# Node marks built tile by tile on VectorE, in the first and the last layer of a graph network

## The chip, the cores and the metric

The kernel runs on one core of a Trainium2 chip. The metric is the device time of one execution in microseconds (us); lower is better. The core's engines work beside each other and meet only at semaphores: TensorE (PE in the profile; PEld is its loading of weights), VectorE (DVE), ScalarE (ACT), GpSimd (POOL), which here issues the indirect DMAs, and SyncE (SP), which issues the others.

## The reference, cut to what matters

Four graph layers run over the same 3125 nodes of width 128 and the same 100000 edges, sorted by destination. Two of them matter here:

```
# layer 0, two steps of:
edge  = concat(h[src], h[dst])
msg   = relu(edge @ mW1 + mb1) @ mW2 + mb2
att   = sigmoid(relu(edge @ aW1 + ab1) @ aW2 + ab2)
agg   = segment_sum(msg * att, dst)          # then a node update
# layer 3, once:
msg   = xW[edge_type, src] * deg_inv[dst]    # 16 relations
out   = segment_sum(msg, dst) + x @ self_loop
```

Layers 1 and 2 use dense blocks of an adjacency matrix that the kernel builds at its start. The change does not touch them.

## The kernel before, in words

Edges lie in tiles of 128, one edge a lane. Four tiles are a quad, and the whole edge list is 202 to 204 quads. In both layers a quad goes through the same steps. GpSimd issues four indirect DMAs, one a tile, each of which fetches 128 rows (one per edge, picked by a list of indices in `stage`) into a `ring` buffer in SBUF. VectorE makes the quad's marks: for every tile a 128x128 matrix `mark` that has a 1 where the lane's destination node, relative to the tile's window (`words[..., D_LOC]`), is the column's number, and 0 elsewhere. TensorE multiplies `mark` (as weights) with the fetched rows and adds to PSUM at the window's columns; this is the segment sum. A semaphore `s_done` counts quads that TensorE has finished and frees their ring slot and mark slot.

`attention_pass` (layer 0, lines 1751 to 1907, run twice, 204 quads each) has a ring of 6 quads. Here VectorE also makes `spread` (L1810), a 128x512 matrix compared from `locs` in bf16 against the lane's number; TensorE multiplies it with the node rows of the destinations (L1871, "expansion", two tiles at a time into one PSUM bank `hid`, two quads ahead of the marks' matmuls); VectorE adds the result to the fetched rows (L1829, one add for two tiles), then forms the attention product of each tile with an accumulator (L1834); ScalarE makes the sigmoid (L1854) and scales the messages (L1860); TensorE sums (L1889, L1891). Because `hid` is one bank, an expansion waits for the add before it, and an add for its expansion. VectorE's order in a quad is: spread of the next quad, marks of this quad, wait for the four DMAs (`s_full`), then add, two products, add, two products. Before each quad TensorE's own sequencer loads 16 register values that say which columns to address (`Where.load`, L1405). ScalarE copies the indices to `stage` when a ring slot's DMAs have landed (L1851), and GpSimd waits for that and for `s_done`.

`last_pass` (layer 3, lines 1631 to 1742, 202 quads) has a ring of 8 quads and far less beside the DMAs: VectorE makes the marks as soon as TensorE has finished with their slot (L1688), and TensorE does four matmuls a quad (L1728).

Both are loops written out by hand, six or eight quads a body. The mark of a quad is one `scalar_tensor_tensor` over 128x512 elements: its inputs are the f32 numbers 0 to 127 (`tile_no`, repeated four times by a step of zero) and the four location words of each lane (repeated 128 times each).

Of the kernel before, what the change touches and what calls it, by code (L numbers as in the profile page):

```python
# [6 lines left out]
F32, I32, BF16, F16 = mybir.dt.float32, mybir.dt.int32, mybir.dt.bfloat16, mybir.dt.float16  # L7
# [3 lines left out]
P = 128  # L11
# [6 lines left out]
QUAD = 4  # L18
# [10 lines left out]
D_LOC, D_SRC, D_T16, D_ROW = 0, 1, 2, 4  # L29
# [1601 lines left out]
def last_pass(k, own, rows, loop, out):  # L1631
# [7 lines left out]
    words, where = k.by_dst, k.where  # L1639
    ring = k.sb("ring", [P, RING * QUAD, D], F32, own)  # L1640
    mark = k.sb("mark", [P, RING, QUAD, P], F32, own)
    stage = k.sb("stage", [P, RING * QUAD], I32, own)
    s_full = [k.sem(f"s_full{q}") for q in range(RING)]
    s_staged, s_mark, s_done, s_go = (k.sem(x) for x in ("s_staged", "s_mark", "s_done", "s_go"))
    s_mm, s_out, s_x, s_dve = (k.sem(x) for x in ("s_mm", "s_out", "s_x", "s_dve"))
# [11 lines left out]
    with nc.Block() as block:  # L1657
        @block.scalar
        def _(eng):
            for q in range(RING):  # L1660
                eng.activation(stage[:, q * QUAD:(q + 1) * QUAD], index(q * QUAD, QUAD), ACT.Copy).then_inc(s_staged, 1)  # L1661
            with eng.Fori(0, bodies) as i:
                for q in range(RING):

                    eng.wait_ge(s_full[q], i * (16 * QUAD) + 16 * QUAD)
                    eng.activation(stage[:, q * QUAD:(q + 1) * QUAD], index(i * body + body + q * QUAD, QUAD),  # L1666
                                   ACT.Copy).then_inc(s_staged, 1)

        @block.gpsimd
        def _(eng):  # L1670
            def quad(i, q):
                eng.wait_ge(s_staged, i * RING + q + 1)

                eng.wait_ge(s_done, i * RING + q + 1)
                eng.sem_inc(s_go, 1)
                for t in range(q * QUAD, (q + 1) * QUAD):
                    eng.indirect_dma_start(ring[:, t, :], None, rows,  # L1677
                                           bass.IndirectOffsetOnAxis(stage[:, t:t + 1], 0)).then_inc(s_full[q], 16)
            every(eng, quad)
            for q in range(RING):  # L1680
                eng.wait_ge(s_full[q], (bodies + (q < rest)) * 16 * QUAD)

        @block.vector
        def _(eng):
            def quad(i, q):
                at = i * body + q * QUAD
                eng.wait_ge(s_done, i * RING + q + 1)
                eng.scalar_tensor_tensor(mark[:, q, :, :], k.tile_no[:, 0:P].unsqueeze(1).to_broadcast([P, QUAD, P]), 0.0,  # L1688
                                         words[:, bass.ds(at, QUAD), D_LOC].unsqueeze(2).to_broadcast([P, QUAD, P]),
                                         ALU.add, ALU.is_equal).then_inc(s_mark, 1)  # L1690

            c = Count(eng, s_dve)
            c.step(eng.tensor_scalar(k.deg[:, :], k.deg[:, :], 1.0, None, ALU.max))
            c.step(eng.reciprocal(k.deg[:, :], k.deg[:, :]))
            for b, c0, n, w0, wn in banks():
                x = k.x[:, w0:w0 + wn, :]
                eng.wait_ge(s_mm, b + 1)
                eng.tensor_tensor(x, x, k.ps[:, FREE, 0:n].rearrange("p (w d) -> p w d", d=D), ALU.add).then_inc(s_x, 1)
            every(eng, quad)

            eng.wait_ge(s_done, RING + NQUADS)
            eng.wait_ge(s_x, NB)
            for b, c0, n, w0, wn in banks():
                for j in range(wn):
                    x = k.x[:, w0 + j, :]
                    last = eng.scalar_tensor_tensor(x, k.ps[:, b, j * P:(j + 1) * P], k.deg[:, w0 + j:w0 + j + 1], x,  # L1706
                                                    ALU.mult, ALU.add)
                last.then_inc(s_x, 1)

        @block.tensor  # L1710
        def _(eng):
            eng.sem_inc(s_done, RING)
            open_banks(k, eng)
            for b, c0, n, w0, wn in banks():
                if b:
                    eng.wait_ge(s_x, b)
                for j in range(wn):
                    last = eng.matmul(k.ps[:, FREE, j * P:(j + 1) * P], k.hT[:, c0 + j * P:c0 + (j + 1) * P], loop[:, :],
                                      start=True, stop=True)
                last.then_inc(s_mm, 1)  # L1720
            tiles = Where(k, eng, where)

            def quad(i, q):
                cols, _ = tiles.load(i * RING + q)
                eng.wait_ge(s_mark, i * RING + q + 1)
                eng.wait_ge(s_full[q], i * (16 * QUAD) + 16 * QUAD)
                for j in range(QUAD):
                    last = eng.matmul(k.psf[:, bass.ds(cols[j], P)], mark[:, q, j, :], ring[:, q * QUAD + j, :], start=False,  # L1728
                                      stop=False, skip_group_check=True)
                last.then_inc(s_done, 1)  # L1730
            every(eng, quad)

        @block.sync
        def _(eng):
            for b, c0, n, w0, wn in banks():
                eng.wait_ge(s_x, NB + b + 1)
                if w0 + wn < NW:
                    eng.dma_start(out[c0:c0 + n, :].rearrange("(w p) d -> p w d", p=P), k.x[:, w0:w0 + wn, :]).then_inc(s_out, 16)
                else:
                    eng.dma_start(out[c0:N, :], k.x[0:TAIL, w0, :]).then_inc(s_out, 16)  # L1740
            eng.wait_ge(s_out, 16 * NB)
# [9 lines left out]
def attention_pass(k, own, rows, here, w_att, b_att):  # L1751
# [8 lines left out]
    mark = k.sb("mark", [P, NQ, QUAD, P], F32, own)  # L1760
    spread = k.sb("spread", [P, NQ, QUAD * P], F32, own)
    locs = k.sb("locs", [P, NQ, QUAD * P], BF16, own)
    stage = k.sb("stage", [P, NQ * QUAD], I32, own)
    dot = k.sb("dot", [P, NQ * QUAD], F32, own)

    att = k.sb("att", [P, NQ * QUAD, 2], F32, own)
# [2 lines left out]
    s_staged, s_mark, s_done, s_go = (k.sem(x) for x in ("s_staged", "s_mark", "s_done", "s_go"))  # L1769
    s_spread, s_exp, s_add, s_dot, s_att, s_msg = (k.sem(x) for x in ("s_spread", "s_exp", "s_add", "s_dot", "s_att", "s_msg"))  # L1770
    s_set = k.sem("s_set")
    words = k.by_dst
# [3 lines left out]
    with nc.Block() as block:  # L1776
# [28 lines left out]
        def _(eng):  # L1805
# [6 lines left out]
            def body(i, last):  # L1812
                for q in range(NQ):
# [4 lines left out]
                    elif not last:  # L1818
                        spread_quad(i + 1, 0, g + 1)
                    eng.wait_ge(s_done, g + 1)  # L1820
                    eng.scalar_tensor_tensor(mark[:, q, :, :], k.tile_no[:, 0:P].unsqueeze(1).to_broadcast([P, QUAD, P]), 0.0,  # L1821
                                             words[:, bass.ds(at, QUAD), D_LOC].unsqueeze(2).to_broadcast([P, QUAD, P]),
                                             ALU.add, ALU.is_equal).then_inc(s_mark, 1)
                    eng.wait_ge(s_full[q], i * (16 * QUAD) + 16 * QUAD)
                    for pair in range(2):
                        t = q * QUAD + pair * 2
# [3 lines left out]
                        for j in (pair * 2, pair * 2 + 1):  # L1830
# [3 lines left out]
                            eng.scalar_tensor_tensor(ring[:, t, D:W2], ring[:, t, D:W2], 0.0, w_att[:, :], ALU.max, ALU.mult,  # L1834
                                                     accum_out=dot[:, t:t + 1]).then_inc(s_dot, 1)
            eng.memset(att[:, :, 1], 1.0).then_inc(s_set, 1)
            eng.sem_inc(s_add, 1)
            spread_quad(0, 0, 0)
            with eng.Fori(0, bodies - 1) as i:
# [578 lines left out]
```

## Time and profile before

| | |
|---|---|
| time, median of 3 runs | 7433.94 us |
| lowest and highest | 7425.34 and 7442.86 us |
| span of the profiled execution, first to last instruction | 6780.1 us |
| own time of the profiled execution | not given with the profile; the median is 653.8 us above the span |
| TensorE busy (PE) | 5024.0 us, 74% of the span |
| VectorE busy | 3111.1 us, 46% |
| GpSimd busy | 2431.9 us, 36% |
| ScalarE busy | 1789.9 us, 26% |
| mean granted clock of TensorE | 0.873 of full speed |
| indirect DMAs of GpSimd | 1632 in the two attention passes, 808 in the last pass |

The profile was taken of one execution. Busy shares are averages over very different stages: the attention passes lie from 1040 to 2117 us and from 2203 to 3254 us, the last pass from 5724 to 6763 us, the layers between them from 3254 to 5724 us. A stage is read by who waits for whom inside it, and by what an engine does between two of its instructions.

### The profile page before, as it was taken

Reading aid. Unit: us, or ns where it says so; the run is one execution under the profiler, and the core shown is the slowest. Engines: PE = TensorE matmul, PEld = TensorE weight load, DVE = VectorE, ACT = ScalarE, POOL = GpSimd, SP = SyncE. Lnnn points to the kernel's source line nnn. Section 1 sums busy time; section 2 is a strip of 40 time slices with the busy share of each in tenths; the row PEclk is TensorE's granted clock in tenths of the full one; section 3 lists DMA queues with packets and bytes.
Section 4 is the critical chain, followed back from the end, with each engine's and each line's share of the span. In section 5 each row is a group of like instructions: output and inputs, shape, how many; then the busy total and the mean of one; then the engine's idle time right before and its main releaser. Section 6 shows DMA issues by size and latency. Waiting matters only on the chain. (4 is left out here: it accounts for less than half of the span.)

```text
span 6780.1 us, 95615 instructions
## 1 busy us (share of the span) xinstructions
PE 5024.0 (74%) x29088; PEld 3414.4 (50%) x29089; DVE 3111.1 (46%) x7292; ACT 1789.9 (26%) x4343; POOL 2431.9 (36%) x2473
## 2 busy tenths in 40 slices
PE   2557767777777777777798999999999997443443
PEld 1435556666665676666544444444444444333333
DVE  6889986666664666666565212112112114111111
ACT  2019983444443444444201001001011012000000
POOL 0000006777773777777100000000000001777776
PEclk7569998999999999999899999999999998555555
DMA  2019984444443444444483553553554524211122
GB/s 79 1 47 328 328 279 133 128 121 125 124 121 80 133 128 130 123 129 126 138 304 131 194 192 133 194 193 131 194 180 146 194 97 167 52 51 51 51 51 55
DMA packets 416540, 942.73 MB, mean 139 GB/s; under 512 B 61857, under 2 KB 272982, under 8 KB 406230
## 3 DMA queue, kind: packets, MB, share of 16 engines
q1 hardware_dynamic: 312150, 672.91, 29.4%
q0 software_dynamic: 104192, 267.02, 14.8%
q8 instruction: 144, 2.36, 0.1%
q14 instruction: 54, 0.44, 0.0%
HBM read 735.13 MB, written 204.56 MB: 139 GB/s over the span
## 5 line engine op out<-in xcount | busy, mean ns | idle before, releaser
L1799 POOL DMA_INDIRECT ring<-rows,stage x1632 | 1629.5, 998 | 1138.4 <-ACT stage L1846 642.0
L1677 POOL DMA_INDIRECT ring<-rows,stage x808 | 792.3, 981 | 2716.8 <-ACT stage L1661 2470.9
L1324 PE MATMUL ps<-strip,trans_part 128*128 128x512 f16 (+1 forms) x8232 | 1606.4, 356 | 23.3 <-DVE trans_part L1241 23.3
L1871 PE MATMUL ps<-here,spread 128*128 x3264 | 949.0, 414 | 545.5 <-DVE spread L1810 283.9
L1324 PEld LDWEIGHTS ps<-strip,trans_part 128*128 128x128 bf16 x8232 | 756.5, 98 | 928.2 <-issue 77.4
L1871 PEld LDWEIGHTS ps<-here,spread 128*128 128x128 f32 x3264 | 569.9, 194 | 662.2 <-issue 615.5
L1829 DVE TENSOR_TENSOR ring<-ring,ps 128x512 f32<-128x512 f32 x816 | 560.6, 687 | 699.3 <-PE ps L1871 540.9
L1728 PE MATMUL ps<-ring,mark 128*128 128x128 f32 x1616 | 414.9, 438 | 612.3 <-DMA ring<-rows,stage 610.7
L1889 PE MATMUL ps<-ring,mark 128*128 128x128 f32 x3264 | 695.0, 300 | 0.0
L1728 PEld LDWEIGHTS ps<-ring,mark 128*128 128x128 f32 x1616 | 357.3, 326 | 669.9 <-issue 669.9
L1233 DVE TENSOR_TENSOR trans<-ps,be 128x512 f32<-128x512 f32 x96 | 66.4, 692 | 1186.4 <-PE ps L1314 1186.4
L1889 PEld LDWEIGHTS ps<-ring,mark 128*128 128x128 f32 x3264 | 572.3, 196 | 45.0
L1688 DVE SCALAR_TENSOR_TENSOR mark<-tile_no,by_dst 128x512 f32<-128x512 f32 x202 | 142.8, 711 | 842.5 <-PE ps L1728 842.4
L1860 ACT ACTIVATE ring<-ring,att 128x128 f32<-128x128 f32 x1632 | 521.4, 390 | 13.3
L1891 PEld LDWEIGHTS ps<-att,mark 128*128 128x128 f32 x3264 | 509.0, 197 | 0.0
L1891 PE MATMUL ps<-att,mark 128*128 128x2 f32 x3264 | 467.8, 213 | 0.0
L1278 ACT ACTIVATE trans_part<-trans 128x512 bf16<-128x512 f32 x100 | 62.9, 629 | 1428.9 <-DVE trans L1233 1366.6
L1834 DVE SCALAR_TENSOR_TENSOR ring<-ring,w_att 128x128 f32<-128x128 f32 x1632 | 414.4, 291 | 28.2
L1854 ACT ACTIVATE att<-dot,b_att 128x4 f32<-128x4 f32 x408 | 121.5, 298 | 1139.7 <-DVE ring L1834 1139.7
L881 ACT ACTIVATE piece<-ps 128x1024 f16<-128x1024 f32 x375 | 303.0, 888 | 24.6 <-PE ps L845 24.6
L1666 ACT ACTIVATE stage<-by_dst 128x4 int32 x200 | 41.6, 208 | 988.7 <-DMA ring<-rows,stage 988.7
L1821 DVE SCALAR_TENSOR_TENSOR mark<-tile_no,by_dst 128x512 f32<-128x512 f32 x408 | 277.4, 680 | 0.0
(332 smaller groups left out, 5093.7 us busy)
## 6 DMA issues: line engine op xcount, KB each, us to landing
strip<-adj SPq DMA_DIRECT2D x392, 800.0 KB, 4.3
adj<-piece SPq DMA_DIRECT2D x120, 640.0 KB, 4.0
locs<-loc_rows SPq DMA_DIRECT2D x420, 128.0 KB, 3.1
ahead<-ahead_piece SPq DMA_DIRECT2D x125, 320.0 KB, 4.1
back<-back_piece SPq DMA_DIRECT2D x125, 320.0 KB, 4.5
sheet<-ahead SPq DMA_DIRECT2D x25, 1600.0 KB, 7.4
sheet<-back SPq DMA_DIRECT2D x25, 1600.0 KB, 7.2
ring<-rows,stage POOLq DMA_INDIRECT x2440, 2.5
```

The costliest lines, as they stand in the source:

```text
L881: eng.activation(piece[:, g % PIECES, :, unit[0] * P:(unit[0] + size) * P].rearrange("p t (e c) -> p t e c", c=HN), psf[:, n % 2 * 2 * BAN ...
L1324: last = eng.matmul(k.ps[:, b, 0:cols], part[:, (step * NW + w) % TABLES, m, t * D:(t + 1) * D], strip[:, at % RING, c0:c0 + cols], start= ...
L1677: eng.indirect_dma_start(ring[:, t, :], None, rows, bass.IndirectOffsetOnAxis(stage[:, t:t + 1], 0)).then_inc(s_full[q], 16)
L1728: last = eng.matmul(k.psf[:, bass.ds(cols[j], P)], mark[:, q, j, :], ring[:, q * QUAD + j, :], start=False, stop=False, skip_group_check=True)
L1799: eng.indirect_dma_start(ring[:, t, :], None, rows, bass.IndirectOffsetOnAxis(stage[:, t:t + 1], 0)).then_inc(s_full[q], 16)
L1821: eng.scalar_tensor_tensor(mark[:, q, :, :], k.tile_no[:, 0:P].unsqueeze(1).to_broadcast([P, QUAD, P]), 0.0, words[:, bass.ds(at, QUAD), D ...
L1829: eng.tensor_tensor(ring[:, t:t + 2, :], ring[:, t:t + 2, :], hid, ALU.add).then_inc(s_add, 1)
L1834: eng.scalar_tensor_tensor(ring[:, t, D:W2], ring[:, t, D:W2], 0.0, w_att[:, :], ALU.max, ALU.mult, accum_out=dot[:, t:t + 1]).then_inc(s_ ...
L1860: eng.activation(ring[:, t, 0:D], ring[:, t, 0:D], ACT.Relu, scale=att[:, t, 0:1]).then_inc(s_msg, 1)
L1871: last = eng.matmul(hid[:, j, :], spread[:, q, t * P:(t + 1) * P], here[:, bass.ds(cols[t] * 2, W2)], start=True, stop=True)
L1889: eng.matmul(k.psf[:, bass.ds(now[j], D)], mark[:, q, j, :], ring[:, q * QUAD + j, 0:D], start=False, stop=False, skip_group_check=True)
L1891: done = eng.matmul(k.psf[:, bass.ds(scalar[j], 2)], mark[:, q, j, :], att[:, q * QUAD + j, :], start=False, stop=False, skip_group_check= ...
```

## The change

Each pass gets a 128x128 bf16 copy of the numbers 0 to 127, `lanes`, made once before its loop. The mark of a quad is then made by four `tensor_scalar` instructions, one a tile, that compare `lanes` with the tile's location word as a per-partition scalar. The output stays f32, and the semaphore `s_mark` is raised once, by the fourth.

```
 # last_pass
+    lanes = k.sb("lanes", [P, P], BF16, own)
-                eng.scalar_tensor_tensor(mark[:, q, :, :], k.tile_no[:, 0:P].unsqueeze(1).to_broadcast([P, QUAD, P]), 0.0,
-                                         words[:, bass.ds(at, QUAD), D_LOC].unsqueeze(2).to_broadcast([P, QUAD, P]),
-                                         ALU.add, ALU.is_equal).then_inc(s_mark, 1)
+                for j in range(QUAD):
+                    last = eng.tensor_scalar(mark[:, q, j, :], lanes[:, :], words[:, bass.ds(at + j, 1), D_LOC], None, ALU.is_equal)
+                last.then_inc(s_mark, 1)
...
+            c.step(eng.tensor_copy(lanes[:, :], k.tile_no[:, 0:P]))
 # attention_pass
+    lanes = k.sb("lanes", [P, P], BF16, own)
-                    eng.scalar_tensor_tensor(mark[:, q, :, :], k.tile_no[:, 0:P].unsqueeze(1).to_broadcast([P, QUAD, P]), 0.0,
-                                             words[:, bass.ds(at, QUAD), D_LOC].unsqueeze(2).to_broadcast([P, QUAD, P]),
-                                             ALU.add, ALU.is_equal).then_inc(s_mark, 1)
+                    for j in range(QUAD):
+                        marked = eng.tensor_scalar(mark[:, q, j, :], lanes[:, :], words[:, bass.ds(at + j, 1), D_LOC], None,
+                                                   ALU.is_equal)
+                    marked.then_inc(s_mark, 1)
...
+            eng.tensor_copy(lanes[:, :], k.tile_no[:, 0:P]).then_inc(s_set, 1)
+            eng.wait_ge(s_set, 2)
```

On VectorE, one quad of the attention loop stands in the program before as follows (ISA rows are the sequencer's address arithmetic).

```order
L1809 ISA
L1810 TENSOR_SCALAR spread<-locs,lane 128x512
L1821 ISA
L1821 SCALAR_TENSOR_TENSOR mark<-tile_no,by_dst 128x512
L1828 REGISTER_ALU
L1829 TENSOR_TENSOR ring<-ring,ps 128x512
```

The same stretch of VectorE in the changed program, where lines have moved by three or four:

```order
L1812 ISA
L1813 TENSOR_SCALAR spread<-locs,lane 128x512
L1825 ISA
L1825 TENSOR_SCALAR mark<-lanes,by_dst 128x128
L1825 ISA
L1825 TENSOR_SCALAR mark<-lanes,by_dst 128x128
L1825 ISA
L1825 TENSOR_SCALAR mark<-lanes,by_dst 128x128
L1825 ISA
L1825 TENSOR_SCALAR mark<-lanes,by_dst 128x128
L1832 REGISTER_ALU
L1833 TENSOR_TENSOR ring<-ring,ps 128x512
```

The marks keep their place between the spread and the first add; one instruction with one address computation becomes four with one each.

On VectorE at the start of the last pass's loop, before the change (`deg` and `x` belong to what precedes the loop):

```order
L1693 TENSOR_SCALAR deg<-deg 128x25
L1694 RECIPROCAL deg<-deg 128x25
L1698 TENSOR_TENSOR x<-x,ps 128x512 x6
L1698 TENSOR_TENSOR x<-x,ps 128x128
L1651 UNCONDITIONAL_BRANCH
L1651 ISA
L1688 ISA
L1688 SCALAR_TENSOR_TENSOR mark<-tile_no,by_dst 128x512
```

The same place on VectorE in the changed program:

```order
L1694 CAST lanes<-tile_no 128x128
L1695 TENSOR_SCALAR deg<-deg 128x25
...
L1652 ISA
L1690 ISA
L1690 TENSOR_SCALAR mark<-lanes,by_dst 128x128
L1690 ISA
L1690 TENSOR_SCALAR mark<-lanes,by_dst 128x128
L1690 ISA
L1690 TENSOR_SCALAR mark<-lanes,by_dst 128x128
L1690 ISA
L1690 TENSOR_SCALAR mark<-lanes,by_dst 128x128
```

The copy to `lanes` stands ahead of the loop, and the four comparisons stand where the one stood. No other engine's order changes.

## Rows read from the trace of the kernel before

**Rows 1.** Groups by line; after the bar: busy us, mean ns; idle before, by releaser.

```profile
L1799 POOL DMA_INDIRECT ring<-rows,stage x1632 | 1629.5, 998 | 1138.4 <-ACT stage L1846 642.0 <-issue 496.2 <-PE ps L1891 0.3
L1677 POOL DMA_INDIRECT ring<-rows,stage x808 | 792.3, 981 | 2716.8 <-ACT stage L1661 2470.9 <-issue 245.6 <-PE ps L1728 0.3
...
L1821 DVE SCALAR_TENSOR_TENSOR mark<-tile_no,by_dst 128x512 f32<-128x512 f32 x408 | 277.4, 680 | 0.0
...
L1688 DVE SCALAR_TENSOR_TENSOR mark<-tile_no,by_dst 128x512 f32<-128x512 f32 x202 | 142.8, 711 | 842.5 <-PE ps L1728 842.4
```

**Rows 2.** Busy by engine in the two attention passes; first number the length.

```profile
1040.00:2117.00 1077.00, 794.21 (x4832) 712.62 (x4831) 701.62 (x2427) 440.79 (x1283) 827.70 (x816) 0.97 0.46 124
2203.00:3254.00 1051.00, 795.16 (x4832) 713.82 (x4831) 697.35 (x2428) 436.26 (x1284) 801.75 (x816) 0.97 0.48 128
```

**Rows 3.** Single lines' instructions: ns minimum/median/maximum, first and last start in us.

```profile
L1799 POOL DMA_INDIRECT ring<-rows,stage x1632: 942/946/1475, 1040.7 to 3252.6; - x182
L1677 POOL DMA_INDIRECT ring<-rows,stage x808: 940/944/1462, 5724.4 to 6761.7; - x162
```

**Rows 4.** Timeline of an attention quad: start, length in us, instruction, [idle before].

```profile
2003.92 1.13 PE L1871 MATMUL ps<-here,spread 128*128 x4 [1.49 <-DVE spread L1810]
...
2008.23 0.58 DVE L1810 TENSOR_SCALAR spread<-locs,lane 128x512 f32<-128x512 bf16 x1
...
2008.74 0.67 DVE L1821 SCALAR_TENSOR_TENSOR mark<-tile_no,by_dst 128x512 f32<-128x512 f32 x1
2008.87 1.36 POOL L1799 DMA_INDIRECT ring<-rows,stage  x1 [0.30 <-issue]
...
2010.51 0.69 DVE L1829 TENSOR_TENSOR ring<-ring,ps 128x512 f32<-128x512 f32 x1 [1.10 <-DMA ring<-rows,stage]
```

**Rows 5.** Timeline of two attention quads in a later stretch.

```profile
2726.91 0.28 DVE L1834 SCALAR_TENSOR_TENSOR ring<-ring,w_att 128x128 f32<-128x128 f32 x1
2727.00 1.02 POOL L1799 DMA_INDIRECT ring<-rows,stage  x1 [0.30 <-issue]
...
2727.72 0.68 DVE L1821 SCALAR_TENSOR_TENSOR mark<-tile_no,by_dst 128x512 f32<-128x512 f32 x1
...
2727.74 1.13 PE L1871 MATMUL ps<-here,spread 128*128 x4 [1.02 <-issue]
...
2728.91 0.69 DVE L1829 TENSOR_TENSOR ring<-ring,ps 128x512 f32<-128x512 f32 x1 [0.50 <-PE ps L1871]
...
2732.06 0.48 DVE L1810 TENSOR_SCALAR spread<-locs,lane 128x512 f32<-128x512 bf16 x1
2732.07 0.95 POOL L1799 DMA_INDIRECT ring<-rows,stage  x1 [0.30 <-issue]
...
2732.66 1.12 PE L1871 MATMUL ps<-here,spread 128*128 x4 [1.00 <-DVE spread L1810]
```

**Rows 6.** Timeline of VectorE and GpSimd where a spread and its marks meet a DMA.

```profile
1358.48 0.48 DVE L1810 TENSOR_SCALAR spread<-locs,lane 128x512 f32<-128x512 bf16 x1
1358.72 1.06 POOL L1799 DMA_INDIRECT ring<-rows,stage  x1 [0.30 <-issue]
1358.87 0.69 DVE L1821 SCALAR_TENSOR_TENSOR mark<-tile_no,by_dst 128x512 f32<-128x512 f32 x1
```

**Rows 7.** Timeline of the last pass, VectorE's marks and the DMAs beside them.

```profile
6298.02 0.69 DVE L1688 SCALAR_TENSOR_TENSOR mark<-tile_no,by_dst 128x512 f32<-128x512 f32 x1 [4.22 <-PE ps L1728]
6298.07 1.46 POOL L1677 DMA_INDIRECT ring<-rows,stage  x1 [0.30 <-issue]
...
6303.54 0.76 DVE L1688 SCALAR_TENSOR_TENSOR mark<-tile_no,by_dst 128x512 f32<-128x512 f32 x1 [4.83 <-PE ps L1728]
6303.58 0.94 POOL L1677 DMA_INDIRECT ring<-rows,stage  x1 [0.30 <-issue]
```

**Rows 8.** Timeline: 25 consecutive 128x128 tensor_scalars elsewhere in the program.

```profile
98.59 4.99 DVE L1448 TENSOR_SCALAR h<-h,stat 128x128 f32<-128x128 f32 x25
```

**Rows 9.** The sequencer's address step ahead of each mark, from the marks' line.

```profile
L1821 DVEq FUSED_REGOPS  x396: 69/69/81, 1043.1 to 3220.8; - x198
```

## The prediction

> **What bounds the kernel now.** I read the busy shares by stage first, then the groups by line, then the timeline inside a quad. The page gives TensorE 74% of the span, but the change lies only in the two attention passes and the last pass, so those are read alone.
>
> In the attention passes GpSimd never rests. It has 816 DMA instructions in each pass, busy 827.70 and 801.75 us [rows 2], and idles 496.2 us over 1629 "issue" gaps, 0.304 us each [rows 1]. 827.70 + 816 x 0.304 = 1076 us against a pass of 1077 us, and 801.75 + 248 = 1050 against 1051 [rows 2]. So the length of a pass is the sum of GpSimd's serial instructions; whatever makes one of them longer makes the pass longer. The last pass is the same: 792.3 + 245.6 = 1037.9 us [rows 1] against 5724.4 to 6761.7 plus the last 0.9, which is 1038 us [rows 3].
>
> What makes them longer? The median instruction takes 0.946 us in the attention passes, but the mean is 0.998; in the last pass 0.944 against 0.981 [rows 1, 3]. The excess is 1629.5 - 1632 x 0.946 = 85.6 us and 792.3 - 808 x 0.944 = 29.5 us, together 115 us. The timeline shows where it sits. In [rows 4] the mark starts at 2008.74 and runs to 2009.41; a DMA instruction starts 0.13 us after the mark's start and takes 1.36 us, 0.41 too long. It starts 2008.87, so the mark ends 0.54 us into it: the DMA instruction seems to want something 0.54 - 0.41 = 0.13 us after its start and gets it when the mark ends. In [rows 7] the mark starts 0.05 us before the DMA instruction, ends 0.64 into it, and the excess is 1.46 - 0.94 = 0.52, again 0.12 short of the overlap. When the mark starts 0.04 us ahead, the DMA instruction is normal (0.94) and the mark is the one that is longer, 0.76 instead of 0.69 [rows 7]. So it is a lock: who comes first holds it, and VectorE holds it for its whole instruction. A 128-wide product that ends 0.19 us into a DMA instruction costs it 0.07 (1.02) [rows 5], which fits the same rule.
>
> The quad of [rows 4] repeats. The first add waits for the DMAs (1.10 us idle), so VectorE follows GpSimd at a fixed distance, the mark always falls on the start of a DMA instruction, and a quad takes about 5.4 us instead of 4 x 1.25 = 5.0. In other stretches, as [rows 5], TensorE sets the pace: expansions start at 2727.74 and 2732.66, 4.92 us apart, and the add waits for TensorE.
>
> **What the change does to this.** *The train of four.* Twenty-five 128x128 tensor_scalars take 4.99 us [rows 8]. With one of them 0.28 long, they start (4.99 - 0.28) / 24 = 0.196 us apart. That row is f32 to f32. I take it for bf16 to f32 too, since the bf16 spread over 512 takes 0.48 [rows 5, 6] against 0.68 for the f32 mark over 512 [rows 1]: it has a faster mode already. So a train takes 3 x 0.196 + 0.28 = 0.87 us instead of 0.68. Lower bound: 0.48, the bf16 spread of the same total width [rows 6]. Upper bound: each as costly as that whole spread, three at 0.40 apart (0.24 from the spread's start to the DMA's and 0.15 on to the mark's, [rows 6]) plus 0.48, 1.68 us. The sequencer's address step of 0.069 us each [rows 9] fits under 0.196. I take 0.87, the row nearest in shape.
>
> The Trainium skill (VectorE: DVE Perf Modes, the section on the trn2 errata) gives 58 cycles plus the elements over the mode's factor at 0.96 GHz. By that estimate four instructions of 128 in a doubled mode would take 0.51 us and one of 512 in plain mode 0.59, so the train would be the shorter one. The measured 0.196 apart says otherwise, and the measurement decides.
>
> *What it costs VectorE.* 0.19 us more per quad, 610 quads. In a quad paced by TensorE the mark starts at 2727.72 and the add at 2728.91 [rows 5], 1.19 us of room against a train of 0.87; in a quad paced by GpSimd 1.77 us [rows 4]. In the last pass VectorE idles over 4 us a quad [rows 7]. So the addition is hidden behind TensorE's expansion and the DMAs. If the room were gone (the upper bound of 1.68), a TensorE-paced quad would be 0.49 us later: that end is kept in the range only through its small chance. Who waits for the marks themselves is TensorE's sum two quads later, which is in no hurry.
>
> *What it gives GpSimd.* The lock is now held for one instruction of 0.28 us. In the locked quad the first of the four starts 0.13 before the DMA instruction [rows 4], ends 0.15 into it, and costs 0.15 - 0.13 = 0.02 instead of 0.41. In the last pass, 0.05 ahead, it ends 0.23 into it and costs 0.10 instead of 0.52. Between two back-to-back VectorE instructions GpSimd does get in: in [rows 6] the spread ends 0.24 into the DMA instruction, the mark has been started by then, and the excess is only 1.06 - 0.95 = 0.11, the rule for the spread's end alone.
>
> *Attention.* Not all of the 85.6 us is the marks'; spreads and products keep theirs (0.11 in [rows 6], 0.07 in [rows 5]). And TensorE is close behind: five quads at 4.92 and one with a longer gap for the loop's branch (1.49 against 1.00, [rows 4, 5]) make (5 x 4.92 + 5.41) / 6 = 5.00 us, the same as GpSimd's 5.00. Two queues of equal pace lose a little to each other. I take 5.07 us a quad where it is (1077 + 1051) / 408 = 5.22 now: 408 x 5.07 = 2068, so 60 us less. Bounds: 85 if everything goes, 20 if TensorE and jitter take most of it.
>
> *Last pass.* 29.5 us at about 0.5 a hit are some 59 hits in 202 quads. At 0.10 or less each they leave 6: 23 us less. Bounds 15 and 29.
>
> *The copies.* `lanes` is made three times in all (twice in the attention passes, once in the last), each under 0.3 us by the single instructions above, plus a wait: 1 us more.
>
> Sum: -60 - 23 + 1 = -82 us. The profiled execution gives no own time; its span of 6780.1 would become 6698, and the median of the runs, 7434, stands 654 us above the span for reasons that the change doesn't touch. I forecast 7352 us.
>
> **The rivals.** *One, slower: the train acts as one hold.* If GpSimd did not get in between the four, the hold would last 0.87: in the locked quad the train ends 0.74 into the DMA instruction and costs 0.61 instead of 0.41, and it is hit 0.87 / 0.68 = 1.28 times as often. 115 x 0.61 / 0.41 x 1.28 = 219 us, 104 more than now, 7538 us. For it: the four are issued with nothing between them. Against it: [rows 6]. It decides once the mean excess per quad passes 115 / 610 = 0.19 us.
>
> *Two, slower: the faster mode blocks more of a DMA instruction than the old one did.* The mark moves from an f32 form with two tensor inputs to the form of the spread. If GpSimd cannot do the later part of its work while such an instruction runs, each train would lengthen the DMA instruction that it lies on wherever it falls. Priced at 0.4 us in each of 610 quads, as a locked one costs today, that is 244 us, 129 more than now, 7563 us. Against it: a spread that runs from 2732.06 to 2732.54, over the first half of the DMA instruction of 2732.07, leaves it at 0.95 [rows 5].
>
> The Trainium skill (SBUF — State Buffer, "Who interferes with whom") speaks for it: a two-port instruction of VectorE and a GpSimd instruction exclude each other entirely, whichever starts first, while one with two SBUF inputs excludes only GpSimd's reads; and it warns that GpSimd can't write DMA descriptors meanwhile. By that rule the new form would contend where the old one did not. Of the first half of the rule the trace shows the part with two inputs: 1.46 against 0.94 in [rows 7].
>
> *Three, faster but little: TensorE takes over in the attention passes at once*, so that only the last pass gains: -22 us, 7412 us. For it: 5.00 against 5.00. Against it: the 5.4 us quads of [rows 4] leave TensorE 0.45 us of room each (the expansion was finished, the add waited for the DMA).
>
> *Four, no change: the excess is not the marks'* but belongs to whatever VectorE runs there, and returns with the four. 7434 us. Against it: the same mark moved by 0.09 us against the DMA changes it from 1.46 to 0.94 [rows 7].
>
> **How the numbers follow.** The forecast 0.65; rival one 0.06; two 0.06; three 0.14; four 0.09. Faster by over 0.2% (15 us, about what a measurement of this kernel can tell from no change): the forecast and three, 0.79. Within 0.2%: rival four and a little, 0.10. Slower: 0.11. The range goes from 7322 (both excesses gone, 7434 - 115 = 7319, nearly) to 7428, which takes in rival three and the start of four.
>
> **What would show it.** GpSimd's DMA instructions: mean near 0.96 in the attention passes and 0.95 in the last, hardly any above 1.2 us. The trains about 0.87 us long. Passes of about 1034 us each and 1015 us. The share of adds that wait for TensorE rises, and that of adds that wait for DMAs falls. Wrong if DMA instructions stay at 1.3 and more under the trains (rivals one and two, told apart by whether the train's first or any of them is at the start), if the DMA mean falls but GpSimd begins to wait for TensorE (rival three), or if the trains last over 1.2 us and adds begin right behind them.

## The result, and the profile after

The changed kernel takes 7494.8 us, median of 5 runs, against 7433.2 for the kernel before: ratio 1.0070, 95% interval 1.0054 to 1.0087. It is slower by 0.7% (the medians alone differ by 62 us, 0.8%); I had forecast 1.1% faster, in a range that ends at 7428.

The profiled execution of the changed kernel took 7465.9 us, its span is 7464.0. So a span stands 2 us below its time, not 654. The profile of the kernel before (6780.1 us) was therefore of an execution some 650 us shorter than those that were timed. The chip that each of them ran on is not on record.

Groups by line of the changed kernel, the columns as in [rows 1], which they answer:

```profile
L1802 POOL DMA_INDIRECT ring<-rows,stage x1632 | 1563.3, 958 | 1764.5 <-issue 1111.6 <-ACT stage L1852 643.5 <-ACT stage L1857 7.3
L1678 POOL DMA_INDIRECT ring<-rows,stage x808 | 765.5, 947 | 2867.5 <-ACT stage L1662 2467.7 <-issue 398.3 <-PE ps L1730 1.5
...
L1825 DVE TENSOR_SCALAR mark<-lanes,by_dst 128x128 f32<-128x128 bf16 x1632 | 363.4, 294 | 0.0
...
L1690 DVE TENSOR_SCALAR mark<-lanes,by_dst 128x128 f32<-128x128 bf16 x808 | 170.8, 294 | 939.0 <-remote 697.0 <-issue 161.2 <-PE ps L1730 80.4
```

GpSimd's DMA instructions are shorter than in [rows 1], as forecast: 0.998 to 0.958 and 0.981 to 0.947 us in the mean. But its idle "issue" time in the attention passes is now 1111.6 us where it was 496.2: it waits, and so it no longer sets the pace. Its instructions (940/946/1203 ns, the answer to [rows 3]) now spread from 1041.1 to 3812.6 us:

```profile
L1802 POOL DMA_INDIRECT ring<-rows,stage x1632: 940/946/1203, 1041.1 to 3812.6; - x182
L1678 POOL DMA_INDIRECT ring<-rows,stage x808: 938/944/1076, 6281.2 to 7445.7; - x162
```

The busy time in the same stretches as [rows 2] says it again: 656 DMAs in the first where all 816 had fitted.

```profile
1040.00:2117.00 1077.00, 725.09 (x3850) 646.47 (x3851) 581.53 (x2424) 342.63 (x1027) 628.35 (x656) 0.85 0.36 100
2203.00:3254.00 1051.00, 724.93 (x3743) 632.43 (x3745) 553.04 (x2257) 336.27 (x986) 558.84 (x584) 0.84 0.34 95
```

The longest waits of VectorE (columns: engine, line, waited for: us in total, times, longest) name a releaser that the table of before did not have. The profile writes "remote" where a semaphore's event fits the end of no instruction on record; this program runs on one core, so no other core can be meant:

```profile
DVE mark L1690 <- remote: 697.0, 53, 20.8
DVE ring L1833 <- remote: 606.8, 123, 8.0
```

And the timeline of an attention quad, the counterpart of [rows 4], shows one of them:

```profile
2000.42 0.88 DVE L1825 TENSOR_SCALAR mark<-lanes,by_dst 128x128 f32<-128x128 bf16 x4
...
2001.10 1.02 POOL L1802 DMA_INDIRECT ring<-rows,stage  x1 [0.30 <-issue]
...
2002.44 1.13 PE L1877 MATMUL ps<-here,spread 128*128 x4
...
2006.25 0.94 POOL L1802 DMA_INDIRECT ring<-rows,stage  x1 [0.30 <-issue]
2008.95 0.69 DVE L1833 TENSOR_TENSOR ring<-ring,ps 128x512 f32<-128x512 f32 x1 [6.11 <-remote]
...
2009.78 1.00 POOL L1802 DMA_INDIRECT ring<-rows,stage  x1 [2.59 <-issue]
2009.78 2.07 PE L1877 MATMUL ps<-here,spread 128*128 x4 [5.43 <-DVE ring L1833]
```

The train of four takes 0.88 us. It ends 0.20 us into the DMA instruction of 2001.10 and costs it 1.02 - 0.95 = 0.07: the forecast's rule, for the new form too. But then the expansion of 2002.44, which should be done by 2003.6, is reported done at 2008.93 (the semaphore's own time in the trace), and VectorE, GpSimd and the next expansion stand behind it. The granted clock falls to the lower of its two levels, 1.2 GHz, at 2008.38, after TensorE has run nothing for 4.0 us, and the next expansion takes 2.07 instead of 1.13 us. I call this a hold of TensorE.

How many there are takes care to count, because this trace also lacks records. It keeps 669 of the expansions' some 820 semaphore events. For 116 of the 816 expansions the event came over 2 us after the end and before the next expansion's end: those are late. For 155 no event of their own is on record: since the next expansion waits for this one's add, its event can't come later than that, so it is missing. 271 expansions with no event within 2 us are thus 116 late ones and 155 gaps in the record. 115 adds waited over 3 us, in the median 26 us apart, which agrees with the 116. VectorE's adds lack events too (191 of 816), but none that is on record is over 1 us late: it is TensorE that is held.

### The profile page after: what moved, and what is told of

Its sections match the earlier page's. It is cut to its first block and busy times, and to the rows that moved or that the text cites. A ratio compares the mean times of both kernels' runs of the same rounds, so it can differ in the third digit from the quotient of the medians.

```text
span 7464.0 us, 99233 instructions
## 1 busy us (share of the span) xinstructions
PE 5262.1 (70%) x29085; PEld 3589.3 (48%) x29089; DVE 3199.8 (43%) x9125; ACT 1770.8 (24%) x4343; POOL 2339.0 (31%) x2473
## 5 line engine op out<-in xcount | busy, mean ns | idle before, releaser
L1802 POOL DMA_INDIRECT ring<-rows,stage x1632 | 1563.3, 958 | 1764.5 <-issue 1111.6
L1877 PE MATMUL ps<-here,spread 128*128 x3264 | 1114.1, 472 | 864.3 <-DVE ring L1833 612.2
L1678 POOL DMA_INDIRECT ring<-rows,stage x808 | 765.5, 947 | 2867.5 <-ACT stage L1662 2467.7
L1877 PEld LDWEIGHTS ps<-here,spread 128*128 128x128 f32 x3264 | 664.8, 226 | 993.8 <-issue 923.0
L1730 PE MATMUL ps<-ring,mark 128*128 128x128 f32 x1616 | 417.1, 407 | 707.4 <-issue 663.0
L1895 PE MATMUL ps<-ring,mark 128*128 128x128 f32 x3264 | 773.8, 327 | 0.0
L1730 PEld LDWEIGHTS ps<-ring,mark 128*128 128x128 f32 x1616 | 326.8, 284 | 797.7 <-issue 796.2
L1895 PEld LDWEIGHTS ps<-ring,mark 128*128 128x128 f32 x3264 | 651.5, 222 | 66.6
L1690 DVE TENSOR_SCALAR mark<-lanes,by_dst 128x128 f32<-128x128 bf16 x808 | 170.8, 294 | 939.0 <-remote 697.0
L1897 PEld LDWEIGHTS ps<-att,mark 128*128 128x128 f32 x3264 | 571.3, 219 | 0.0
L1897 PE MATMUL ps<-att,mark 128*128 128x2 f32 x3264 | 503.8, 224 | 0.0
L1825 DVE TENSOR_SCALAR mark<-lanes,by_dst 128x128 f32<-128x128 bf16 x1632 | 363.4, 294 | 0.0
```

What stands on the lines that cost most here:

```text
L1678: eng.indirect_dma_start(ring[:, t, :], None, rows, bass.IndirectOffsetOnAxis(stage[:, t:t + 1], 0)).then_inc(s_full[q], 16)
L1802: eng.indirect_dma_start(ring[:, t, :], None, rows, bass.IndirectOffsetOnAxis(stage[:, t:t + 1], 0)).then_inc(s_full[q], 16)
L1825: marked = eng.tensor_scalar(mark[:, q, j, :], lanes[:, :], words[:, bass.ds(at + j, 1), D_LOC], None, ALU.is_equal)
L1877: last = eng.matmul(hid[:, j, :], spread[:, q, t * P:(t + 1) * P], here[:, bass.ds(cols[t] * 2, W2)], start=True, stop=True)
L1895: eng.matmul(k.psf[:, bass.ds(now[j], D)], mark[:, q, j, :], ring[:, q * QUAD + j, 0:D], start=False, stop=False, skip_group_check=True)
L1897: done = eng.matmul(k.psf[:, bass.ds(scalar[j], 2)], mark[:, q, j, :], att[:, q * QUAD + j, :], start=False, stop=False, skip_group_check= ...
```

## The experiments

Ratios are against the kernel before on the same chip, with 95% intervals. The chips have numbers; 4, 5, 7, 11 and 13 came up, each at one time only. "Late" and "without a record" are counted as above.

**Where the loss lies: before again, and each half of the change alone.** On chip 4. `b1_before` is the kernel before unchanged; `b2_att_only` has the diff's lines in `attention_pass` alone, `b3_last_only` those in `last_pass` alone:

```
# b2: attention_pass; b3: last_pass
-    eng.scalar_tensor_tensor(mark[:, q, :, :], <tile_no x4>, 0.0, <words x128>, ALU.add, ALU.is_equal)
+    for j in range(QUAD):
+        eng.tensor_scalar(mark[:, q, j, :], lanes[:, :], words[:, bass.ds(at + j, 1), D_LOC], None, ALU.is_equal)
```

> The kernel before, unchanged. The changed kernel's trace (span 7464 us) has what the shown trace of before (span 6780 us, against a median of 7434) lacks: VectorE standing still for some 3 to 8 us every 26 us of an attention pass, between two records, with nothing to wait for (123 adds, 607 us in all). Theory A (the stalls are a state of the execution and not of the change: the shown trace was of an execution that had none, the timed executions of before have them too): this trace has a span near 7430 us, attention passes of about 1330 us each instead of 1077 and 1051, and stalls of VectorE in them. Theory B (the change brings the stalls): the span is near 6780 us again with passes near 1060 us, and the 650 us between span and time lie outside the span.

> Only the attention passes make their marks tile by tile; the last pass is as before. Theory A1 (instruction supply: VectorE's stalls come after a fixed number of its instructions, and the attention loop now has 6 more instructions in each quad): this one alone carries most of the change's +61 us, +40 to +70 us. Theory A2 (the loss lies in the last pass): within 15 us of before, or faster by the 60 us forecast for the attention passes.

> Only the last pass makes its marks tile by tile; attention is as before. In it VectorE goes from 3 to about 9 instructions a quad. Theory A1 (stalls counted by instructions): slower by up to 60 us if the last pass' stalls grow with its instructions, since each stall there is not hidden; the original forecast, which knew no stalls: 23 us faster.

The kernel before took 6798.0 us here, and its copy 6784.3 (0.9978, 0.9954 to 1.0002): the same kernel that was timed at 7433. Its trace has a span of 6816.2 for a run of 6817.9, and no "remote" wait. So theory A's stalls did not show, nor did theory B's 650 us outside the span; what differs is the chip, or the time at which it was used. The attention half took 6711.2 us (0.9869, 0.9851 to 0.9887), the last-pass half 6753.0 (0.9940, 0.9915 to 0.9964). Theories A1 and A2 both failed here in their losses: both halves gain, 87 and 45 us (24 to 58 by the second's interval) against the 60 and 23 forecast. DMA instructions in the attention half:

```profile
L1800 POOL DMA_INDIRECT ring<-rows,stage x1632 | 1559.3, 955 | 1137.8 <-ACT stage L1850 641.2 <-issue 474.9 <-ACT stage L1855 20.1
L1677 POOL DMA_INDIRECT ring<-rows,stage x808 | 791.7, 980 | 2714.8 <-ACT stage L1661 2468.8 <-issue 245.7 <-PE ps L1728 0.3
```

The attention group is at 955, the untouched last pass still at 980.

**Both halves, on a chip without holds.** On chip 5, the changed kernel and the one before, both as they are.

> The changed kernel, unchanged, beside the kernel before on the same chip. The runs with before at 6798 us had the attention passes alone at 0.987 and the last pass alone at 0.994 of before, without VectorE's stalls. Theory C1 (the two parts add up and the result of 1.007 belongs to executions with stalls, in which before takes 7433 us): where before takes about 6800 us, this one takes 0.981 of it, some 6670 us; where before takes about 7430, 1.007 of it and its trace has the stalls. Theory C2 (both parts together bring the stalls, neither does alone): about 7490 us even where before takes 6800.

> The kernel before, for its trace. Theory C1: if it takes about 7430 us here, its trace has VectorE stalls of 4 to 6 us in the attention passes as the changed kernel's had, and fewer than its 123; if about 6800, none. Theory C2: no stalls at any time.

6673.3 against 6808.1 us, ratio 0.9796 (0.9780 to 0.9812). C1 holds, C2 falls. The first fence is the changed kernel, the second the kernel before, both by line:

```profile
L1802 POOL DMA_INDIRECT ring<-rows,stage x1632 | 1558.8, 955 | 1137.2 <-ACT stage L1852 640.6 <-issue 476.8 <-ACT stage L1857 19.5
L1678 POOL DMA_INDIRECT ring<-rows,stage x808 | 763.2, 945 | 2713.2 <-ACT stage L1662 2467.3 <-issue 245.6 <-DMA ring<-rows,stage 0.3
L1833 DVE TENSOR_TENSOR ring<-ring,ps 128x512 f32<-128x512 f32 x816 | 560.9, 687 | 538.4 <-PE ps L1877 529.5 <-DMA ring<-rows,stage 8.1
```

```profile
L1799 POOL DMA_INDIRECT ring<-rows,stage x1632 | 1640.2, 1005 | 1137.3 <-ACT stage L1846 640.9 <-issue 496.5
L1677 POOL DMA_INDIRECT ring<-rows,stage x808 | 804.2, 995 | 2713.4 <-ACT stage L1661 2467.5 <-issue 245.3 <-PE ps L1728 0.3
L1829 DVE TENSOR_TENSOR ring<-ring,ps 128x512 f32<-128x512 f32 x816 | 560.6, 687 | 707.2 <-PE ps L1871 516.8 <-DMA ring<-rows,stage 190.3
```

GpSimd's busy time fell by 1640.2 - 1558.8 + 804.2 - 763.2 = 122 us, and the time by 135. Adds waited 8.1 instead of 190.3 us for DMAs. No expansion is late or without a record, in either trace.

**Which part of the change does it.** On chip 7: four f32 instructions (`d1`), one with bf16 numbers (`d2`), two f32 of 256 (`d3`), and the changed kernel (`d4_after`), in both passes.

```
# d1 (n = 1) and d3 (n = 2), in place of the tensor_scalar
+    for j in range(0, QUAD, n):
+        eng.scalar_tensor_tensor(mark[:, q, j:j + n, :], <tile_no x n>, 0.0, words[:, bass.ds(at + j, n), D_LOC]..., ALU.add, ALU.is_equal)
# d2
+    eng.scalar_tensor_tensor(mark[:, q, :, :], lanes[:, :].unsqueeze(1).to_broadcast([P, QUAD, P]), 0.0, <words x128>, ALU.add, ALU.is_equal)
```

> The change's splitting alone: four 128-wide scalar_tensor_tensors in f32 instead of one of 512, no bf16 and no doubled mode. Theory D1 (a DMA instruction is held up by whichever VectorE instruction with two SBUF inputs runs when it starts, until that one ends, so only the length of one instruction counts): GpSimd's DMA mean falls to about 0.957 us in attention and 0.947 in the last pass as with the changed kernel, ratio to before 0.979 to 0.984 where before takes about 6800 us. Theory D2 (the gain comes from the bf16 input or the doubled mode): ratio near 1.00. Where before takes about 7430 us, this one has the changed kernel's instruction count and takes 1.00 to 1.02 of before under the theory that the stalls go with VectorE's instructions.

> The change's bf16 lane numbers alone: one 512-wide scalar_tensor_tensor that reads lanes in bf16. Theory D1: the instruction stays at about 0.68 us and so does the hold: ratio 0.995 to 1.005, DMA means near 1.01 and 0.99 as before. Theory D2: 0.98. Instruction count as before, so where before takes about 7430 us also 1.00.

> Two 256-wide scalar_tensor_tensors a quad. Each lasts about 0.42 us. Theory D1: started 0.05 us ahead of a DMA instruction, one costs 0.42 - 0.05 - 0.13 = 0.24 instead of 0.52 us, and 0.16 instead of 0.41 in the locked attention quad, so a bit over half of the changed kernel's gain: ratio 0.987 to 0.991 where before takes about 6800. Where before takes about 7430 it adds 2 VectorE instructions (one with its address step) a quad instead of 6, and stalls less than the changed kernel.

> The changed kernel once more on the chip of these three, as their measure: 0.980 of before where before takes about 6800 us, 1.007 where it takes about 7430.

This chip is of the other kind: before took 7392.1 us. d1 1.0048 (1.0030 to 1.0065), d2 1.0007 (0.9995 to 1.0018), d3 1.0034 (1.0020 to 1.0049), the changed kernel 1.0048 (1.0030 to 1.0066). The bf16 input alone does nothing; splitting alone, without the faster mode, costs what the whole change costs. Every trace has holds: 109 to 123 late expansions (133 to 189 more without a record), 115 of them with the single instruction of d2. So the holds are not brought by VectorE's instruction count, as I had thought when I wrote A1; d3, which was to have fewer than the changed kernel, has 123 against 114. To read the DMA instructions one needs the kernel before on such a chip. Its attention passes, unchanged, are in `f1_no_fetch` on chip 13 (the last experiment). The groups are d2's, d1's and then f1's:

```profile
L1802 POOL DMA_INDIRECT ring<-rows,stage x1632 | 1593.5, 976 | 1672.9 <-issue 1026.0 <-ACT stage L1851 646.0 <-PE ps L1896 0.9
...
L1824 DVE SCALAR_TENSOR_TENSOR mark<-lanes,by_dst 128x512 f32<-128x512 bf16 x408 | 279.2, 684 | 0.0
```

```profile
L1804 POOL DMA_INDIRECT ring<-rows,stage x1632 | 1565.0, 959 | 1700.9 <-issue 1055.3 <-ACT stage L1855 640.7 <-ACT stage L1860 3.4
...
L1827 DVE SCALAR_TENSOR_TENSOR mark<-tile_no,by_dst 128x128 f32<-128x128 f32 x1632 | 366.0, 285 | 0.0
```

```profile
L1798 POOL DMA_INDIRECT ring<-rows,stage x1632 | 1595.9, 978 | 1702.9 <-issue 1057.8 <-ACT stage L1845 644.2 <-PE ps L1890 0.9
```

GpSimd waits over 1000 us in all three. With holds the DMA instruction of the kernel before is 0.978 us in the mean, not 1.00, and 83 of 1632 last over 1.2 us instead of 199 on chip 5: VectorE and GpSimd meet less often. One long instruction with bf16 leaves it there (0.976), four short f32 ones bring it to 0.959, as the changed kernel does on the same chip (0.960). So D1 holds against D2 for the DMA instruction, though not for the ratio of 0.98, since no chip without holds came up for these. D1's size for d3 was missed: two instructions of 256 were to give over half of the gain, and the mean is 0.976, as with one, although only 7 DMA instructions last over 1.2 us against d2's 72. Why is open.

**The train moved away from the first add.** On chip 11.

```
 # attention_pass, marks of the changed kernel
-    for j in range(QUAD):
+    for j in range(2):                      # between spread and first add
...
+    if pair == 0:                           # behind the first add's two products
+        for j in (2, 3):
+            marked = eng.tensor_scalar(mark[:, q, j, :], lanes[:, :], words[:, bass.ds(at + j, 1), D_LOC], None, ALU.is_equal)
+        marked.then_inc(s_mark, 1)
```

> The changed kernel, but in the attention passes only two of the four comparisons stay between the spread and the first add; the other two stand behind the first add's two products, where VectorE waits 0.76 us for the second expansion. On chip 7, where TensorE is held for some 5 us again and again and GpSimd is not the bound, the changed kernel took 1.005 of before, and 109 first adds started right behind the marks against 84 with one instruction. Theory E1 (there the loss is the longer train ahead of those adds): the train ahead of the add falls from 0.87 to 0.48 us, below the single instruction's 0.68, so this version takes 0.996 to 1.000 of before where before takes about 7400 us, 20 to 50 us less than the changed kernel. Theory E2 (the loss comes with more instructions or more starts of them, wherever they stand): 1.005 again. Where before takes about 6800 us GpSimd's DMAs set the pace and both theories say 0.979 to 0.983.

> The changed kernel on the same chip as the version with the split train, as its measure: 0.980 of before where before takes about 6800 us, 1.005 where it takes about 7400. A third state of affairs would count against the division into two kinds of chip.

Before 7445.7, changed 7492.2 (1.0065, 1.0049 to 1.0080), split train 7471.0 (1.0031, 1.0019 to 1.0043). The timeline of the split version right after a hold:

```profile
1604.17 0.69 DVE L1831 TENSOR_TENSOR ring<-ring,ps 128x512 f32<-128x512 f32 x1 [1.68 <-issue]
...
1605.01 1.13 PE L1880 MATMUL ps<-here,spread 128*128 x4
...
1605.33 0.48 DVE L1813 TENSOR_SCALAR spread<-locs,lane 128x512 f32<-128x512 bf16 x1
...
1605.72 0.48 DVE L1825 TENSOR_SCALAR mark<-lanes,by_dst 128x128 f32<-128x128 bf16 x2
...
1606.17 0.69 DVE L1831 TENSOR_TENSOR ring<-ring,ps 128x512 f32<-128x512 f32 x1
```

The expansion of 1605.01 ended at 1606.14, since it came without the 1.0 us of register loads ahead of it (no idle time stands in its row), and the add starts 0.03 us later, as the two marks end too. The short train just fits. A train of four from 1605.72 would have ended at 1606.59, some 0.4 us behind the expansion: there VectorE's train is on the path. In the changed kernel 98 first adds start within 0.1 us of the marks' end, in the split version 44. Theory E1 has the direction and 21 us, the low end of its 20 to 50; its 0.996 to 1.000 was missed. E2 falls as the whole of the loss, but 25 of the 47 us remain with the split train, and for them it is open.

**What the holds need.** On chip 13, the kernel before with another last pass. `f1_no_fetch` fills the ring on GpSimd, `f2_plain_dma` fetches consecutive rows from SyncE; both leave the gather of the last layer out. Each was run once.

```
 # f1, GpSimd
-    eng.indirect_dma_start(ring[:, t, :], None, rows, ...).then_inc(s_full[q], 16)
+    eng.memset(ring[:, t, :], 1.0).then_inc(s_full[q], 16)
 # f2, GpSimd's loop removed; SyncE, behind the same two waits
+    eng.dma_start(ring[:, t, :], rows[t * P:(t + 1) * P, :]).then_inc(s_full[q], 16)
```

> The kernel before, but the last pass fetches no rows: GpSimd fills each tile of the ring with ones instead of issuing its indirect DMA (the output of that layer is left out). The attention passes are as before. On chips 7 and 11 TensorE's semaphores came over 2 us late some 270 times in the attention passes and the last pass was 105 to 160 us longer, while all stages without GpSimd's indirect DMAs took the same time to 10 us on every chip. Theory F1 (the holds need GpSimd's software DMAs): on such a chip the last pass without them has no holds, TensorE's quads following each other without gaps in which nothing is waited for. Theory F2 (the holds come with this kind of matmul or loop of TensorE's, whatever is fetched): holds remain. On a chip where before takes about 6800 us neither is told apart.

> The kernel before, but in the last pass SyncE issues plain DMAs of 128 consecutive rows to the ring in place of GpSimd's indirect ones (the gather by edge is left out): the same bytes land, and GpSimd does nothing. Theory F1: on a chip where before takes about 7400 us the last pass has no holds and is set by SyncE's issues. Theory F3 (the holds come with the landing DMA traffic): they remain. On a chip where before takes about 6800 us neither is told apart, but both kernels still show how fast TensorE and VectorE go through the pass when GpSimd's 1.25 us per tile are gone.

Before took 7445.0 us in its one run, f1 6616.9, f2 6686.6. Their attention passes, unchanged, have holds (127 and 126 late expansions). In their last passes all 202 quads' `s_done` are on record and none is over 1 us late; with GpSimd's indirect DMAs on chip 7 (d2) 57 of 202 are, and for 77 more no event stands before the next quad's end. On chip 5 none is late or missing. From TensorE's first to its last matmul the last pass took 329 and 388 us against 1117 in d2. By line, the last pass of f2:

```profile
L1718 PE MATMUL ps<-ring,mark 128*128 128x128 f32 x1616 | 264.9, 316 | 124.3 <-DMA ring<-rows 73.7 <-DVE mark L1678 38.5 <-issue 11.2
...
L1678 DVE SCALAR_TENSOR_TENSOR mark<-tile_no,by_dst 128x512 f32<-128x512 f32 x201 | 138.4, 692 | 235.0 <-PE ps L1718 235.0
```

VectorE's marks wait for TensorE alone, not for "remote". F1 holds, F3 falls for plain DMAs: the same bytes from SyncE's queue bring no hold. F2 falls. The comparison with f1 and f2 is inside one trace each, so it does not hang on the chip; but f2 changes the queue and the addresses (consecutive instead of scattered rows) together, and both last passes run about three times as fast.

The semaphore events kept in the traces draw the same line. They are missing only where the holds are:

| semaphore events kept | attention passes | last pass | everything else |
|---|---|---|---|
| kernel before, chip 5 (`c2`) | 19946 and 19945 | 13515 | 23131 |
| changed kernel, the timed result | 7375 and 7358 | 2252 | 23012 |
| plain DMAs in the last pass, chip 13 (`f2`) | 7818 and 7745 | 13012 | 23439 |

In f2's last pass the events come at 34 per us, against 19 and 13 in the passes of chip 5, and are kept. So missing records and holds come together, with the indirect DMAs. Which brings which isn't shown: a cause behind both is possible, and so is a recording that holds TensorE up on these chips. Every execution on record, timed ones too, comes with the span and clock of a recording, so no run here shows the time without one.

## Why the prediction was wrong, point by point

**The step that failed** is the last sentence of the sum: that the median "stands 654 us above the span for reasons that the change doesn't touch". Those 654 us lay inside the attention and last passes, in the executions that were timed: the kernel before's own attention passes take 1329 and 1326 us in f1 on chip 13, against the 1076 and 1050 that I had read. In the trace after, GpSimd's DMAs of the two attention passes and the last pass stretch over some 1335, 1349 and 1164 us, on chip 5 over 1027, 1028 and 1009, while the stages outside them agree within some 10 us. The profile that I read was of an execution without holds, and what bound it was not what bound the timed ones. So the two terms of the sum, -60 for attention and -23 for the last pass, were taken for a bound that wasn't there; in their place stands a loss of 62 us. It isn't seen in the last pass, where GpSimd's DMAs stretch over 1154.7 us with the changed kernel on chip 7 and 1154.9 with d2, but in the attention passes (2635 against 2620 us together, one trace each).

**"GpSimd never rests"** was right for that trace ([rows 1, 2]) and for chips 4 and 5. With holds it waits 1111.6 - 496.2 = 615 us more in the attention passes; DMA instructions that are shorter there by 66 us against [rows 1], or 33 against the kernel before with holds (1595.9 in f1), only make it wait longer. The gain of 82 us went there.

**The lock and its arithmetic** stood up for the start of a DMA instruction. Train: 0.87 forecast, 0.87 measured in the median, up to 1.09. DMA means: near 0.96 and 0.95 forecast, 0.955 and 0.945 on chip 5. Passes: 1034 and 1015 forecast, 1027 and 1009 measured. GpSimd gets in between two back-to-back instructions. The gain without holds was 135 us rather than 82: the attention part 87 on chip 4 where I took 60, and the last pass part 45 where I took 23. I had left 13 us for jitter between the two engines that did not come: the passes shrank to GpSimd's own 816 x (0.955 + 0.304) = 1027 us, 5.04 us a quad instead of 5.07. The rest is that the kernel before has more hits in other executions (means of 1.016 and 1.005 us in attention on chips 4 and 5, 0.991 and 0.995 in the last pass) than in the trace shown (0.998 and 0.981).

**What the lock left out.** The two forms differ in a second part of a DMA instruction. Each line is one kernel's marks, ns minimum/median/maximum: before in the trace shown, and the changed kernel on chip 5.

```profile
L1821 DVE SCALAR_TENSOR_TENSOR mark<-tile_no,by_dst x408: 671/681/745, 1043.5 to 3256.8; 128x512 f32<-128x512 f32 x136
```

```profile
L1825 DVE TENSOR_SCALAR mark<-lanes,by_dst x1632: 266/280/501, 1043.2 to 3187.9; 128x128 f32<-128x128 bf16 x182
```

An old mark that starts 0.50 to 0.60 us into a DMA instruction takes its usual 0.68 us (16 cases). A new one takes 0.40 us in the mean instead of 0.28 (332 cases), and the spread, 0.48 us long, then ends 1.19 us after the DMA instruction's start whether it started 0.50 or 0.65 into it, as if it could begin only 0.71 us in. The other way round, a DMA instruction on which a spread starts 0.30 to 0.40 us in takes 1.01 to 1.04 us instead of 0.95 (40 cases in the trace of [rows 1]). The forecast had no term for either; both are small beside what the change gives.

**"The addition is hidden behind TensorE's expansion"** failed with holds. After a hold the next expansion comes without the wait for register loads, and about 100 first adds follow the marks at once: 100 x 0.19 = 19 us as an estimate. Moving half of the train away takes 0.39 us from it, up to 100 x 0.39 = 39 us by the same estimate, and gave 21 back. That is part of the loss of 34 us (chip 7), 47 (chip 11) and 62 (the timed result). The rest is open; d3 (1.0034) and d1 (1.0048) only say that splitting costs something here: their intervals overlap, and they don't separate the number of instructions from the train's length.

**The rivals.** One (the train as one hold) is refuted by the DMA means. Two (a faster mode blocks more) is refuted in its size, not in kind. The Trainium skill (SBUF — State Buffer, "Who interferes with whom") says that VectorE in a two-port mode and a GpSimd instruction shut each other out for the whole instruction, whichever comes first, and that an instruction with two SBUF inputs contends only with what GpSimd reads. The traces agree that the faster form meets GpSimd where the old one did not (0.40 against 0.28 us, and 1.01 to 1.04 against 0.95, above), but for parts of a DMA instruction, not the whole of it. The part on two SBUF inputs agrees (1.46 against 0.94 us in [rows 7], and 122 us less over 2440 DMA instructions on chip 5 once VectorE's instructions there are short). Three (TensorE takes over) came nearest: TensorE did, but through holds, and with a loss. Four falls with d1 (0.959 us) against d2 and the kernel before with holds (0.976, 0.978). No rival had an engine that stands still for a reason outside the program, though 654 us that no row explained was the place to look.

**Open:** what holds TensorE on chips 7, 11 and 13 and not on 4 and 5, and whether it is the chip, as each came up at one time only, or the recording. The traces show that the holds come only with GpSimd's indirect DMAs, and nothing of how.

## What to carry to other kernels

Compare the profile's span with the timed median before anything else: a profiled run's span is 2 us short of its time, so a gap of 9% means that the profile is of another condition, and its bound may not be the one that counts. Before counting late events in a trace, count how many events it kept. In this kernel an instruction with two SBUF inputs on VectorE delayed a GpSimd DMA instruction that started under it until it ended, so splitting it in four was worth 2% where GpSimd set the pace; the bf16 input had no part in the shorter DMA instruction (0.959 us without, 0.960 with it), but the 2% were measured only with it. Where GpSimd didn't set the pace, a loss of 0.5 to 0.7% remained. If a kernel gathers through GpSimd, time it on several chips.

## What the hardware showed that I had not expected

On chips 7, 11 and 13 TensorE's completions come late again and again while GpSimd issues indirect DMAs: in the attention passes mostly by 2 to 5 us, every 20 to 26 us in the median, and in the last pass by up to 10 us and more. It makes this kernel 9% slower; on chips 4 and 5 it never happens. During such a hold TensorE's sequencer goes on in steps of about 0.7 us instead of about 0.1. The register arithmetic of `Where.load` shows it, ns minimum/median/maximum, in the changed kernel of the timed result and then on chip 5:

```profile
L1406 PEldq FUSED_REGOPS  x1018: 2/95/1412, 1041.1 to 7444.4; - x170
```

```profile
L1406 PEldq FUSED_REGOPS  x1018: 95/95/176, 1040.4 to 6656.3; - x170
```

A mark that begins 0.04 us before a DMA instruction is itself delayed (0.76 instead of 0.69), one that begins 0.05 us before delays the DMA instruction by 0.52 [rows 7].
